# Text norms of groups 2 and 3 issued one pass earlier, and the rotation's sum ahead of the row numbers and patch rows in VectorE's order

## What is computed

```python
tokens = einsum('bpi,hi->bph', patches, W) + b            # 64 patches an image
h = concat([class_token, tokens]) * pos_embed             # 65 rows
h = concat([h, txt], axis=1)                              # 65 + 128 = 193 rows of 128
x = layernorm(h)
q, k = elu(x @ Wqk + bqk) + 1, split                      # 8 heads of 16
q_r, k_r = rope(q), rope(k)                               # f*cos + swapped(f)*sin
kv = einsum('bhnd,bhne->bhde', k_r * scale, v * scale)    # v is x
out = einsum('bhnd,bhde->bhne', q_r, kv) * z              # z = 1 / (q . mean k)
h = h + out + conv3(x)
x2 = layernorm(h)
h = h + moe(x2)      # 8 experts, the best 2 of each row, plus one shared expert
```

## Time and profile before

| | us |
|---|---|
| runs of the kernel | 251.96, 252.32, 253.23 (median 252.32) |
| the profiled execution | 254.19 |
| its span, first to last instruction | 252.3 |
| TensorE busy (matmul) | 223.3 (89%) |
| VectorE busy | 190.1 (75%) |
| ScalarE busy | 155.8 (62%) |
| GpSimd busy | 114.7 (45%) |
| mean granted clock of TensorE | 0.967 of full speed |
| start of L950 in passes 1 to 6 | 31.77, 46.89, 59.05, 71.48, 83.64, 95.83 (by the chain that ended last) |

### The profile page before, as it was taken

How to read it: one execution, slowest core, us unless ns; L and a number is a source line. 1 busy time by engine, 2 the same in 40 slices (tenths; PEclk the granted TensorE clock), 3 DMA queues, 4 the chain that set the end, 5 groups by cost and what they waited for, 6 DMA issues and landing times.

```text
span 252.3 us, 5578 instructions
## 1 busy us (share of the span) xinstructions
PE 223.3 (89%) x1477; PEld 191.5 (76%) x1485; DVE 190.1 (75%) x741; ACT 155.8 (62%) x438; POOL 114.7 (45%) x122
## 2 busy tenths in 40 slices
PE   3888879999899999988989979999999999999930
PEld 2768779989798989766576657888888888887720
DVE  3548896999999999988986778666666666665892
ACT  3056575676876867849863266666666666666390
POOL 1400000084837483803667703666666666666400
PEclk9999995999999999979999999999999999999995
DMA  6999981060607010100113331423332232329666
GB/s 189 353 360 355 328 315 62 0 232 26 233 24 243 22 56 22 42 10 13 55 42 93 79 83 34 115 62 100 92 89 81 84 94 83 90 81 275 159 157 190
DMA packets 31565, 31.68 MB, mean 126 GB/s; under 512 B 4338, under 2 KB 27419, under 8 KB 30768
## 3 DMA queue, kind: packets, MB, share of 16 engines
q1 hardware_dynamic: 27240, 24.57, 32.5%
q0 software_dynamic: 3392, 6.36, 7.7%
q10 hardware_dynamic: 904, 0.41, 0.6%
HBM read 22.80 MB, written 9.03 MB: 126 GB/s over the span
## 4 chain that ended last, share of the span: by engine, by line
PE 60%; DVE 24%; ACT 6%; issue 4%; DMA 2%; SPq 1%; DVEq 0%; ACTq 0%
PE bank L1621 15%; PE bank L1641 10%; PE bank L1630 5%; PE bank L1539 3%; PE bank L1333 3%; PE bank L1524 3%; PE bank L1527 3%; DMA cst<-in_consts 2%; DVE st L842 2%; PE bank L1610 2%; PE bank L1402 2%; PE bank L1416 2%; DVE sh_h L1103 2%; DVE att L908 2%; DVE att L899 2%
## 5 line engine op out<-in xcount | busy, mean ns | idle before, releaser
L813 POOL DMA_INDIRECT xs_dram<-xd,pos_i x50 | 55.4, 1109 | 69.7 <-DVE pos_i L1002 56.9
L824 POOL DMA_INDIRECT y_dram<-att,goal x56 | 55.1, 985 | 37.3 <-ACT att L749 37.0
L1333 PE MATMUL bank<-wt,xp_both 128*128 128x128 f32 x288 | 39.6, 290 | 5.7 <-DMA xp_both<-in_patches 5.4
L1333 PEld LDWEIGHTS bank<-wt,xp_both 128*128 128x128 f32 x288 | 37.3, 202 | 7.3 <-DMA xp_both<-in_patches 5.9
L735 ACT ACTIVATE att<-bank 128x256 f32<-128x256 f32 x56 | 21.5, 384 | 24.4 <-PE bank L1621 24.0
L1240 DVE CAST xsT_h<-bank 128x128 fp32r<-128x128 f32 x56 | 16.3, 291 | 24.4 <-PE bank L1610 24.4
L1641 PE MATMUL bank<-w_sb,att 128*128 x224 | 34.7, 277 | 0.0
L1641 PEld LDWEIGHTS bank<-w_sb,att 128*128 128x128 f32 x224 | 29.4, 191 | 0.5 <-issue 0.2
L1621 PE MATMUL bank<-xp_both,xsT_h 128*128 x56 | 26.8, 479 | 0.8 <-DVE xsT_l L1242 0.8
L1253 DVE TENSOR_TENSOR att<-att,bank 128x256 f32<-128x256 f32 x56 | 23.0, 411 | 1.7 <-ACT att L735 1.7
L1621 PE MATMUL bank<-xp_both,xsT_l 128*128 x56 | 22.2, 396 | 0.0
(11 more groups left out here) (212 smaller groups left out, 498.7 us busy)
## 6 DMA issues: line engine op xcount, KB each, us to landing
xp_both<-in_patches SPq DMA_DIRECT2D x6, 1152.0 KB
xs_all<-xs_dram SPq DMA_DIRECT2D x56, 64.5 KB, 1.8
xd<-y_dram SPq DMA_DIRECT2D x8, 384.0 KB, 4.8
w<-in_w SPq DMA_DIRECT2D x2, 1024.0 KB, 11.3
y_dram<-att,goal POOLq DMA_INDIRECT x56, 2.3
xs_dram<-xd,pos_i POOLq DMA_INDIRECT x50
xp_both<-in_patches SPq DMA_DIRECT2D x1, 768.0 KB, 5.6
hrow<-in_txt SPq DMA_DIRECT2D x2, 384.0 KB, 6.9
```

What stands on the lines that cost most here:

```text
L813: nc.gpsimd.indirect_dma_start(out=xs_dram[:, :], out_offset=bass.IndirectOffsetOnAxis(ap=pos_i[0:rows, j, k:k + 1], axis=0), in_=xd[0:row ...
L824: nc.gpsimd.indirect_dma_start(out=y_dram[:, :], out_offset=bass.IndirectOffsetOnAxis(ap=goal[u][:, 0:1].bitcast(I32), axis=0), in_=ys[u][ ...
L1333: M(ps[:, 0:D], xp[p][:, k, :], wt[:, k, :], start=(k == 0), stop=False)
```

## The change

Two things move, and no operation is added, removed or altered. First, `rstd_texts`, `mean_texts` and `norm_texts` for the texts of groups 2 and 3 (only group 2 in `norm_texts`) go from pass 1 to the straight code before the loops. Second, in each pass of VectorE `turn_parts` is split into `sine_part` and `cosine_part`, `mean2` goes between the two, `turn` comes right behind the cosine, and `positions` goes from ahead of `mean2` to behind `patch_stats`.

```diff
@@ scalar
             inverse(0)
             columns1(1)
+            rstd_texts(3, 2, 4)
+            norm_texts(2)
             for i in range(1, G - 1):
...
                 rstd2(i - 1)
-                if i == 1:
-                    rstd_texts(3, 2, 4)
                 if i == 3:
                     rstd_texts(4, 4, G)
-                norm_texts(i + 1)
+                if i > 1:
+                    norm_texts(i + 1)
                 norm2(i - 1)
@@ vector
             attended(0)
             mixed(0)
+            mean_texts(3, 2, 4)
             text_stats(4)
             text_stats(5)
...
                 elu_rest(i)
+                sine_part(i)
+                mean2(i - 1)
+                if i == 3:
+                    mean_texts(4, 4, G)
+                cosine_part(i)
+                turn(i)
+                patch_rows(i + 1)
+                patch_stats(i + 1)
                 if i >= 2:
                     positions(i - 2)
-                mean2(i - 1)
-                if i == 1:
-                    mean_texts(3, 2, 4)
-                if i == 3:
-                    mean_texts(4, 4, G)
-                turn_parts(i)
-                patch_rows(i + 1)
-                turn(i)
-                patch_stats(i + 1)
                 tap_before(i)
```

More of the change, by code:

```diff
@@ L892, in elu_rest, with sine_part @@
                                        op0=ALU.min, op1=ALU.max).then_inc(ftb_done, 1)
-            def turn_parts(g):
+            def sine_part(g):
                 dve.wait_ge(fta_done, g + 1)
@@ L900, in turn_parts, with cosine_part @@
                                 sinx[:].rearrange("p t (h a e) -> p (t h) a e", a=2, e=HD // 2), ALU.mult)
+            def cosine_part(g):
                 V.tensor_tensor(cc[:], ft[:], cosx[:], ALU.mult).then_inc(cs_done, 1)
@@ L1047, in _ @@
             elu_rest(0)
-            turn_parts(0)
+            sine_part(0)
+            cosine_part(0)
             turn(0)
@@ L1128, in _ @@
             elu_rest(G - 1)
-            turn_parts(G - 1)
+            sine_part(G - 1)
+            cosine_part(G - 1)
             second_rows(G - 2)
```

## The result

The changed kernel takes 257.15 us (median of four runs, 255.31 to 257.59); the kernel before, with one run more than in the table of before, took 252.60 (251.96 to 253.23). The ratio is 1.0168, with a 95% interval of 1.0119 to 1.0217: slower by 4.55 us, where 3.5 were forecast. The profiled execution is the quickest of the changed kernel, with 255.31 around a span of 253.5 us, only 1.2 us over that of before.

A forecast was written before the change was run, and what follows sets the result against it. TensorE and VectorE were taken to bound a full pass, neither with more than half a microsecond of room. Pass 1's -0.37 plus 3.88 in passes 2 to 6 took 252.32 to 255.8 us; 8-in-10 range 252.3 to 258.2.

The forecast's parts named there:

- The wait that hadn't shown binds: Passes 2 to 6: TensorE's transposes of xd would wait for VectorE's later `prod` and begin 1.23 us later (pass 4).
- The rival on the other side: Transposes of xd need only the previous pass's `prod`: a pass takes 11.92 us, the whole 250.6 us; chance 0.07.
- The sum's gain is worth nothing there: Pass 4: the rotation's sum starts at 75.36 against 75.95, but `sums` can't use it behind the late transposes.
- L953 to L1434, 5.72: Pass 4: from the pass's start to the transposes of xd, released by `prod` at 77.20, takes 5.72 us.
- L1434 to the next L953, 7.30: From the transposes of xd to the next pass takes 7.30 us, including what queues behind; a pass takes 13.02 us.
- Passes 2 to 5: Longer by 0.86, 0.66, 0.86 and 0.83 us, from the late transposes of xd.
- Pass 6, 0.67: Pass 6 leads into straight code where VectorE waits for `sums` alone, so it loses 0.67 us.
- Pass 1, -0.37: Pass 1: with the text norms gone, xd starts at 34.75 in place of 35.12, a gain of 0.37 us.
- The median: Whole kernel: 255.8 us; bounds 3.1 and 4.4 on the loss in passes 2 to 6 give 255.0 to 256.7.
- What was costed at nothing: Patch rows' offsets and `tap_before` behind `positions` stay hidden, 0.61 us without cover; GpSimd's scatter starts some 3.6 us later.
- The clock: TensorE's two clock falls, costed at 2.0 and 1.3 us; the main forecast, chance 0.45, left them unchanged.
- the second rival: Both clock falls, in pass 1 and at 110 to 112, go: +3.51 - 3.3, so 252.5 us; chance 0.13.

The follow-up runs named there:

- e4: Changed kernel with the counts that `prod` reads for groups 0 to 4 in another bank, so the transposes needn't wait for `prod`: 252.83 us, ratio 1.0023.
- e7: Changed kernel with ScalarE's two rstd operations of the next patch rows (`rstd1`) ahead of its x2T copy: 257.05 us, ratio 1.0186.
- e6: Changed kernel with `positions`, and so `prod`, moved one operation further back, behind the convolution's tap (`tap_before`): 262.14 us, ratio 1.0394.
- e1: Kernel before with only the text norms of groups 2 and 3 moved ahead of the loops, VectorE's order as before: 251.43 us, ratio 0.9976.
- f3: Changed kernel with `prod` alone back ahead of the sine and its three reductions behind the next pass's second tap: 251.50 us, ratio 0.9973.
- e5: Changed kernel with `prod` alone back ahead of the sine, the three reductions left late in the pass: 252.21 us, ratio 0.9989.
- f1: Kernel before with the texts moved, `prod` early, and its three reductions in the next pass behind `tap_behind`: 250.84 us, ratio 0.9943.
- e2: Changed kernel with the text norms back in pass 1, so only VectorE's new order against the kernel before: 257.02 us, ratio 1.0210.

## Why the prediction was right, step by step

- **The wait that hadn't shown binds.** Right: L1434 is released by `prod` in five passes, and L1407's wait is gone. The rival on the other side, that L1434 needs an earlier `prod`, falls by the same rows.
- **The sum's gain is worth nothing there.** Right: it is ready 1.33 us ahead of the L1407 that uses it. More is true: e4 gave the sum its way, and the pass still was 0.3 longer than before. The prediction had it that the wait ahead of L1402, 0.45, is what an earlier rotation could win. That was wrong: the keys' copies would still have waited for the patch rows' offsets, and an earlier sum alone had next to nothing to win. VectorE's room was misread too: in a full pass it is 0.95 us (12.16 less 11.21), not half a microsecond; no term of the sum uses it.
- **L953 to L1434, 5.72.** Measured 5.89 (76.79 - 70.90). The two signalling times were too small: the sine starts 0.10 after `elu_rest` ends (chain of the changed kernel, 72.83 to 72.93), where I took 0.02, and L1434 follows the start of `prod` by 0.31, where 0.23 was reckoned. The upper bound, 0.1 a pass for these, covers more than half of the 0.17.
- **L1434 to the next L953, 7.30, read from pass 3 of before.** Measured 7.24. Right, with what queues behind it: the timeline of pass 4 shows copy, norm and offsets late one after the other, and e7 takes 0.35 of it away by reordering ScalarE alone.
- **Passes 2 to 5.** Predicted 0.86, 0.66, 0.86, 0.83 (3.21); measured 0.96, 0.78, 0.97, 0.93 (3.64).
- **Pass 6, 0.67.** This term was mis-sized: 0.92. I had counted only the delay of `sums` there; the pass lost as much as a full one. Its offsets count as in the others: they begin 6.33 us into the pass before and 7.31 after, and the stretch from them to the next L950 or L953 is 7.93 before, 7.87 after, and 7.86 to 7.98 in eight of the eleven kernels.
- **Pass 1, -0.37.** This was reckoned from L944, ahead of the pass. From there (L947 at 29.20 in the changed kernel) to L1434 it is 7.39 us (36.59 - 29.20), before 7.68 (36.74 - 29.06): -0.29. The wait on xd is 1.25, predicted 1.16. The whole sum is then -0.29 + 3.64 + 0.92 = 4.27, where 3.51 was forecast, and a little above the upper bound of 4.4 less 0.37; at equal clock, without falls, the spans differ by 4.3.
- **The median.** 257.15 lies above the forecast's own range of 255.0 to 256.7, and inside the wide one. Of the 0.76 us by which the sum is short, 0.43 are the signalling times and the like in passes 2 to 5, 0.25 pass 6 and 0.08 pass 1.
- **What was costed at nothing.** The offsets of the patch rows behind `positions` were hidden in this kernel, as predicted: VectorE is idle 0.53 us ahead of them. The cover was L1434 itself. In e4, where L1434 isn't late, it is gone, and the pass is 0.3 longer than before; the prediction's price without cover was 0.61. GpSimd's scatter began 6.52 us into pass 4 (77.42), before 2.82 (74.30), so 3.7 later for 3.6, and no wait of TensorE is on it.
- **The clock.** The main forecast held it unchanged; that the median came near it is in part luck, since the falls weren't unchanged. In the profiled execution both falls are gone, as the second rival had it, and its price, put at 3.3, came to 2.5 + 1.0, of which the texts' move is a part. In the four executions beside it the clock fell too, where isn't known. The Trainium skill, "TensorE: Matmul & The Clock Gate", section "HAM oscillation — how this bites in real kernels", says that a loop whose waits let the clock drop pays in each turn. The trace doesn't show that here: five waits of 1.26 to 2.01 us, each pass at 1.00, and in e6 and e7 one fall among passes 2 to 5, in each of which L1434 waits 1.27 to 2.54 us.

What stays open: where the fall of the four other executions of the changed kernel lies, and what lets it come in one execution and not in the next. In e1, f3 and e5, profiled at a mean clock of 0.980 to 0.982, the only fall ahead of the last 8 us stands where the second one of before stood, between 106 and 114 us. That stretch takes 9.32 to 9.39 us in the seven traces with a fall there and 8.36 or 8.37 in the five without. For the changed kernel this isn't shown, and its four spans are 1.6 to 2.2 us over the profiled one, more than this 1.0.

## What to carry to other kernels

A wait that never shows in a trace still has a slack: before an operation moves later, look up in the order who waits for it, and compare its present end with when that wait is reached (here 73.53 against 75.97). On an engine that runs its list in order, what is ready early gained nothing behind something that was made late; and a bank shared between a result still to be read and the next transposes turned a late reader into a stalled TensorE, which e4 undid. Look for the one operation from which the next turn keeps a fixed distance over several versions: here it was ScalarE's copies of the keys, in nearly every version behind a 0.16 us row of offsets. Freeing VectorE ahead of both of their inputs (f1) gave what the earlier sum alone did not.

## What the runs showed of the hardware

One kernel's executions differ in large part by falls of the clock: the kernel before has spans of 248.7 to 250.0 at a mean clock of 0.988 or 0.989 and of 251.9 to 253.3 at 0.967 or 0.968, so up to 4.6 us, as much as the whole loss measured here. One more took 1230.9 at a clock of 1.00, without a trace. Neither the length of a wait nor its place alone decided whether a fall came: 1.53 was followed by one in both profiles of before, 1.88 in e6 and 2.01 in e7, but 2.0 in pass 1 of e2, 2.01 in the changed kernel and 2.54 in pass 2 of e6 were not. A fall cost between 1.0 us (behind pass 6) and 3.1 (pass 2 of e7, 15.88 against the 12.78 of its pass 4), so a change of half a per cent in this kernel is to be read from the passes at full clock and not from the median.
